# Values of three last expert tiles over the matrix engine, half of the output sums on TensorE and ScalarE, and moved spreads, scale and stores

## What is computed

```python
h = layernorm_gamma_beta(real(fft2(maxpool2(relu(pointwise(depthwise_conv7(x)))))))   # (4, 512, 192)
h = h + linear_attention_taylor2(layernorm(h))                                        # 12 heads of 16
z = layernorm(h)
probs = softmax(z @ Wg + bg)                      # 8 experts, top-1
ffn   = top_p * (gelu(z @ W1[e] + b1[e]) @ W2[e] + b2[e])
v     = clip(ffn @ Wv + bv, -3, 3)                # one value per token
mask  = scores >= 204th largest of sigmoid(z @ Wm + bm)   # per batch, 204 = int(512 * 0.4)
gr,gi = diag((T(v) - i)^-1)                       # T tridiagonal over a batch's 512 tokens
out   = h + ffn + bk_scale * (clip([gr, gi] * mask, -10, 10) @ Wo + bo)
```

## Time and profile before

| what | us |
|---|---|
| median of 3 runs (lowest, highest) | 423.71 (422.89, 426.29) |
| the profiled execution: its own time | 424.41 |
| the profiled execution: its span | 422.5 |
| TensorE busy in the span | 374.3 (89%) |
| VectorE busy | 281.7 (67%) |
| ScalarE busy | 160.3 (38%) |
| mean granted TensorE clock | 0.931 |

### The profile page before, as it was taken

How to read it: one execution, slowest core, us unless ns; L and a number is a source line. 1 busy time by engine, 2 the same in 40 slices (tenths; PEclk the granted TensorE clock), 3 DMA queues, 4 the chain that set the end, 5 groups by cost and what they waited for, 6 DMA issues and landing times. The chain is left out here.

```text
span 422.5 us, 7775 instructions
## 1 busy us (share of the span) xinstructions
PE 374.3 (89%) x2642; PEld 252.8 (60%) x2647; DVE 281.7 (67%) x901; ACT 160.3 (38%) x321; POOL 103.3 (24%) x154
## 2 busy tenths in 40 slices
PE   7999899699998998989998889899599999997273
PEld 4476538133773354733577228798599999996251
DVE  3698843899688996886333773667426656657883
ACT  1001131595317843178531781663233443441000
POOL 2000030251303612036210262201524433421000
PEclk9999999699999999999996799999889999999555
DMA  8674049400685015810179906310511211112504
GB/s 263 193 207 147 0 130 255 125 3 2 189 223 150 2 38 155 220 52 1 55 217 247 391 2 217 115 52 16 181 32 48 53 47 53 46 40 55 168 1 149
DMA packets 26900, 47.94 MB, mean 113 GB/s; under 512 B 11044, under 2 KB 21860, under 8 KB 25332
## 3 DMA queue, kind: packets, MB, share of 16 engines
q1 hardware_dynamic: 21412, 32.73, 25.4%
q10 hardware_dynamic: 2288, 7.15, 6.7%
q0 software_dynamic: 3168, 7.65, 6.3%
HBM read 36.84 MB, written 10.68 MB: 112 GB/s over the span
## 5 line engine op out<-in xcount | busy, mean ns | idle before, releaser
L681 ACT ACTIVATE probs<-ring,ones 128x1024 f32<-128x1024 f32 (+2 forms) x72 | 66.3, 970 | 16.4 <-PE ring L1561 15.0
L606 POOL TENSOR_SCALAR_AFFINE_SELECT probs<-probs 128x256 f32<-128x256 f32 (+1 forms) x72 | 41.5, 581 | 111.2 <-ACT probs L681 111.1
L1707 PE MATMUL att<-w,probs 128*128 x276 | 49.5, 330 | 1.8 <-DVE probs L1184 1.7
L1707 PEld LDWEIGHTS att<-w,probs 128*128 128x128 f32 x276 | 44.7, 192 | 2.8 <-issue 2.7
L1561 PE MATMUL ring<-w1b 128*128 128x256 bf16 (+3 forms) x188 | 39.5, 321 | 7.5 <-ACT probs L681 3.5
L835 DVE SCALAR_TENSOR_TENSOR wide<-w,wdw,wide 128x512 f32<-128x512 f32 x60 | 44.1, 778 | 0.8
L1573 PE MATMUL att<-probs,va 128*32 128x512 f32 (+3 forms) x384 | 39.6, 454 | 2.6 <-POOL probs L606 2.1
L1561 PEld LDWEIGHTS ring<-w1b 128*128 128x128 bf16 x192 | 13.1, 101 | 38.3 <-ACT probs L681 26.5
L632 POOL DMA_INDIRECT ffn_by_token<-probs,target_i x23 | 22.3, 970 | 55.9 <-DVE probs L1193 48.0
L781 ACT ACTIVATE probs<-ring,q_area 128x128 f32<-128x128 f32 x72 | 19.9, 374 | 31.7 <-PE ring L1697 13.5
L622 POOL DMA_INDIRECT pooled<-x_by_token,source_i x23 | 22.9, 993 | 36.8 <-issue 20.6
(11 more groups left out here) (367 smaller groups left out, 707.4 us busy)
## 6 DMA issues: line engine op xcount, KB each, us to landing
w1b<-k_parts ACTq DMA_DIRECT2D x16, 384.0 KB, 10.4
w1b<-q_parts SPq DMA_DIRECT2D x16, 384.0 KB, 8.7
w<-in_w SPq DMA_DIRECT2D x1, 4608.0 KB
w1a<-in_w1a SPq DMA_DIRECT2D x1, 3072.0 KB, 11.0
w<-in_x SPq DMA_DIRECT2D x4, 512.0 KB, 3.7
w<-in_x SPq DMA_DIRECT2D x8, 256.0 KB, 5.0
q_parts<-q_area SPq DMA_DIRECT2D x12, 128.0 KB, 2.6
k_parts<-k_area POOLq DMA_DIRECT2D x12, 128.0 KB, 2.6
```

Of the source, the lines that this page charges most:

```text
L606: nc.gpsimd.affine_select(diag, diag, [[0, len(UNITS[n][1])], [1, P]], ALU.is_ge, minus_one, base=0, channel_multiplier=-1).then_inc(p_rea ...
L681: nc.scalar.activation(squares(n), bank[:, :, 0:N - P * j], ACT.Square, bias=ones[:, 0:1], scale=0.25).then_inc(sq_done, 1)
L1707: last = nc.tensor.matmul(att[2][:, 0:D], hT[slot][:, c, :], w2[:, bass.ds((e * HC + c) * D, D)], start=(c == 0), stop=(c == HC - 1))
```

## The change

It has five parts.

1. `LAST_TILES = 3`: tiles 20, 21 and 22 (before: 21 and 22) bring their values over TensorE. `IN_DRAM` becomes 20, so that the load of `v_raw` waits for one store less and the stores of three tiles stand behind its landing.
2. The three spreads stand in the iterations 18, 19 and 20 of VectorE's loop, each after that iteration's `count_higher` (before: two, in iterations 20 and 21). The third one stands ahead of the mask.
3. The scaling of `wof` moves from behind the scan's levels to the place ahead of them. A copy of one column, after a settle on VectorE's own steps, tells TensorE that `h_all` is complete (`rows_added`).
4. The ten matmuls on zeros ahead of the row product go. In their place TensorE multiplies the second halves of `h_all` by the identity into the four banks `sums_of[1, 3, 5, 7]`, and the four later products are added to that. The banks are dealt out anew.
5. VectorE adds the four first halves alone, SP stores them. ScalarE copies the four second halves out of the banks and issues their stores, two after two copies.

```diff
@@ line 52 of before @@
 YS = 4
+LAST_TILES = 3
 EARLY = TT - NT
@@ line 277 of before @@
         target_i = sb("target_i", [P, SLOT_TILES], I32)
-        lane_of, step_of = sb("lane_of", [P, 2]), sb("step_of", [P, 2])
+        lane_of, step_of = sb("lane_of", [P, LAST_TILES]), sb("step_of", [P, LAST_TILES])
         b2 = oT[:].rearrange("p g n -> p (g n)")
@@ line 312 of before @@
-        sums_of = [ring[0][:, 0, :], ring[0][:, 1, :], ring[1][:, 0, :], ring[1][:, 1, :],
-                   att[0], att[1], att[2], misc]
+        sums_of = [att[0], ring[0][:, 0, :], att[1], ring[0][:, 1, :],
+                   att[2], ring[1][:, 0, :], misc, ring[1][:, 1, :]]
@@ line 330 of before @@
         lane_ids = cnt[:].rearrange("p e t -> p (e t)")
-        own_lane = [ap[:].rearrange("p e t -> p (e t)") for ap in (incl, excl)]
-        own_value = [key[:].rearrange("p t e -> p (t e)")[:, LCH * i:LCH * i + LCH] for i in range(2)]
+        own_lane = [ap[:].rearrange("p e t -> p (e t)") for ap in (incl, excl)] + [probs[:, 3 * S:3 * S + P]]
+        own_value = [key[:].rearrange("p t e -> p (t e)")[:, LCH * i:LCH * i + LCH] for i in range(LAST_TILES)]
+        assert at + 2 * HID <= 3 * S
         assert 2 * B * CH == E * TT
@@ line 413 of before @@
         ft_done, out_ready = sem("feature_terms_done"), sem("output_ready")
+        rows_added, second_ready = sem("expert_rows_added"), sem("second_halves_ready")
@@ line 428 of before @@
-        IN_DRAM = SLOT_TILES - 2
+        IN_DRAM = SLOT_TILES - LAST_TILES
         assert SURE == 5 and SURE % 2 == 1
@@ line 473 of before @@
-        def store_out(eng, odd):
-
-            for i in range(2):
-                for b in range(odd, B, 2):
-                    eng.wait_ge(out_ready, B * i + b + 1)
-                    first = NT * b + 2 * i
-                    eng.dma_start(t["out"][P * first:P * first + 2 * P, :].rearrange("(n p) d -> p n d", p=P),
-                                  h_all[:, first:first + 2, :]).then_inc(s_out, 16)
+        def store_out(eng, first, batches):
+
+            rows = t["out"].rearrange("(b n p) d -> p b n d", p=P, n=NT)
+            tokens = h_all[:].rearrange("p (b n) d -> p b n d", n=NT)
+            for b in batches:
+                eng.dma_start(rows[:, b, first:first + 2, :], tokens[:, b, first:first + 2, :]).then_inc(s_out, 16)
@@ line 572 of before @@
                              ).then_inc(s_ffn[b], 16)
-            store_out(sp, 0)
+            for b in range(B):
+                sp.wait_ge(out_ready, b + 1)
+                store_out(sp, 0, (b,))
             sp.wait_ge(s_out, 16 * 2 * B)
@@ line 806 of before @@
             pair(LAST_PAIR, last=True)
-            store_out(act, 1)
+            for b in range(B):
+                act.wait_ge(ft_done, B + b + 1)
+                nc.scalar.activation(h_all[:, NT * b + 2:NT * b + 4, :].rearrange("p t d -> p (t d)"),
+                                     sums_of[2 * b + 1][:, 0:2 * D], ACT.Copy).then_inc(second_ready, 1)
+                if b % 2:
+                    act.wait_ge(second_ready, b + 1)
+                    store_out(act, 2, (b - 1, b))
@@ line 1255 of before @@
                     count_higher(i - SURE)
-                if i >= IN_DRAM - 1:
-                    spread(i + 1)
+                if IN_DRAM - 2 <= i < IN_DRAM - 2 + LAST_TILES:
+                    spread(i + 2)
                 if i == SURE + TT - 1:
@@ line 1305 of before @@
+            dve.wait_ge(s_wof, 16)
+            st.mark(V.tensor_scalar(wof, wof, scale3[:, 0:1], None, ALU.mult))
             for i in range(LEVELS):
@@ line 1312 of before @@
                 hb = h_all[:, NT * i:NT * i + NT, :]
-                st.mark(V.tensor_tensor(hb, hb, x2_all[:, NT * i:NT * i + NT, 0:D], ALU.add))
-
-            dve.wait_ge(s_wof, 16)
+                ins = V.tensor_tensor(hb, hb, x2_all[:, NT * i:NT * i + NT, 0:D], ALU.add)
+                st.mark(ins)
+
             dve.wait_ge(s_rows, 16)
             dve.wait_ge(s_mask, 16)
-            st.mark(V.tensor_scalar(wof, wof, scale3[:, 0:1], None, ALU.mult))
+            st.settle()
+            nc.vector.tensor_copy(nz[:, 0:1], h_all[:, 0, 0:1]).then_inc(rows_added, 1)
             st.mark(V.tensor_tensor(mask_q, mask_l[:, None, :].to_broadcast([B * CH, 4, LCH]),
@@ line 1377 of before @@
             V.tensor_scalar(f_rows, misc[:, 0:P], onecol[:, 0:1], None, ALU.add).then_inc(rows_copied, 1)
-            for i in range(2):
-                for b in range(B):
-                    dve.wait_ge(ft_done, B * i + b + 1)
-                    hb = h_all[:, NT * b + 2 * i:NT * b + 2 * i + 2, :]
-                    V.tensor_tensor(hb, hb, sums_of[2 * b + i][:, 0:2 * D].rearrange("p (t d) -> p t d", d=D),
-                                    ALU.add).then_inc(out_ready, 1)
+            for b in range(B):
+                dve.wait_ge(ft_done, b + 1)
+                hb = h_all[:, NT * b:NT * b + 2, :]
+                V.tensor_tensor(hb, hb, sums_of[2 * b][:, 0:2 * D].rearrange("p (t d) -> p t d", d=D),
+                                ALU.add).then_inc(out_ready, 1)
@@ line 1764 of before @@
             nc.tensor.matmul(att[1][:, 256:256 + LCH], both_ways, v_raw[0:B * CH, :], start=True, stop=False)
-            for i in range(2):
+            for i in range(LAST_TILES):
                 pe.wait_ge(lane_ready, i + 1)
-                last = nc.tensor.matmul(att[1][:, 256:256 + LCH], own_lane[i], own_value[i], start=False, stop=(i == 1))
+                last = nc.tensor.matmul(att[1][:, 256:256 + LCH], own_lane[i], own_value[i], start=False,
+                                        stop=(i == LAST_TILES - 1))
             last.then_inc(lanes_turned, 1)
@@ line 1786 of before @@
-            keep_clock(WARM_ROWS)
+            pe.wait_ge(rows_added, 1)
+            for b in range(B):
+                nc.tensor.matmul(sums_of[2 * b + 1][:, 0:2 * D], ident[:],
+                                 h_all[:, NT * b + 2:NT * b + 4, :].rearrange("p t d -> p (t d)"), start=True, stop=False)
             pe.wait_ge(feat_ready, 1)
@@ line 1798 of before @@
                     last = nc.tensor.matmul(sums_of[2 * b + i][:, 0:2 * D], f_rows[rows, :],
-                                            wof[rows, 2 * D * i:2 * D * i + 2 * D], start=True, stop=True)
+                                            wof[rows, 2 * D * i:2 * D * i + 2 * D], start=(i == 0), stop=True)
                     last.then_inc(ft_done, 1)
```

## The result

| | kernel before | changed kernel |
|---|---|---|
| median of 18 runs each, alternating (us) | 423.15 | 426.61 |
| ratio to before, 95% interval | | 1.0109 (1.0068 to 1.0151) |
| profiled execution: own time, span | 424.41, 422.5 | 427.26, 425.4 |
| from tile 18's take-out to the end of the span | 51.14 | 54.81 |

The change costs about 1.1%, some 4.6 us. The ratio is taken over each kernel's runs within 1.5% of its fastest run; the medians of all runs are 3.46 us (0.8%) apart. The forecast was 429.1 us, with 424.3 to 430.9 as range, and slower by over 1% as the likeliest outcome.

The account below looks back on a forecast made before the run. TensorE was taken to bound while tiles are made, VectorE behind them, the last 31 us at half clock. Terms 2.6 - 0.25 + 2.5 + 0.6 = 5.4 us on a median of 423.71 gave 429.1, range 424.3 to 430.9.

Parts of the forecast that it names:

- The whole is wrong if the time is under 427: Sign set for the whole forecast of 429.1 us: a measured time under 427 would refute it.
- Term 3 [is wrong] if the clock row shows more than 0.50 before the row product: Sign for the identity products' cost: it assumed TensorE at half clock until the row product.
- Term 1: Spreads and values of the last tiles: later mask and `v_raw` let VectorE start the lanes later, +2.6 us (1.7 to 2.8).
- takes 2.21: TensorE's down product ahead of tile 22's take-out: begins at 388.29, lasts 2.21 us, tile 22 taken at 390.75.
- so the load is late last: Ahead of the lanes: tile 22's value there by 392.7, `v_raw` used at 392.17, its load setting VectorE's start at 393.54.
- Term 2: Scaling moved ahead of the scan's levels, hidden in VectorE's wait, plus a one-column copy: -0.25 us (-0.5 to 0).
- Term 3: Identity products ahead of the row product: eight passes, 5.1 us at half clock, 2.6 hidden by the features' wait: +2.5 us.
- the first rival: TensorE's clock comes back under the identity products: +1.3 us, 425.0; chance 0.24 for early or midway.
- a rise only at the end of the identity products: Late form of the returning TensorE clock: +4.35 us, 428.1; chance 0.24 shared with the early return.
- Term 4: Output, first output product to end: last store issued after 6.1 us instead of 5.5, +0.6 us (-0.4 to +1).
- The reload of ffn: Reload behind three stores, 4.1 us later: no cost forecast; rival has it bind, up to 1.2 us, 430.3, chance 0.08.
- the spreads fit after all: Rival: VectorE's spreads make the mask late by less than a microsecond, lanes no later: +2.6 us, 426.3, chance 0.12.

Follow-up runs that it names:

- e4: Changed kernel with twenty matmuls on zeros in TensorE's wait ahead of down(22); ratio 1.0041 to the kernel before.
- e7: e6 with ScalarE's four copies in a row and the stores shared out between SP and ScalarE; ratio 0.9951 to the kernel before.
- e8: e7 with sixty matmuls on zeros in TensorE's idle time ahead of the scan; ratio 0.9956 to the kernel before.
- e5: Changed kernel with the mask ahead of the third spread and twenty matmuls on zeros ahead of down(22); ratio 1.0007 to the kernel before.
- e6: e2 with two of the four identity products in place of the fourteen matmuls on zeros ahead of the flip; ratio 0.9981 to the kernel before.
- e10: Kernel before with twenty matmuls on zeros instead of fourteen ahead of the flip; ratio 0.9973.
- e1: Kernel before with part 1 of the change alone: three tiles over TensorE, three spreads in iterations 18 to 20; ratio 1.0104.
- e11: e7 with its two spreads in iterations 18 and 20, the second behind the mask; ratio 0.9901 to the kernel before.
- e2: Changed kernel with part 1 undone: two tiles over TensorE, spreads where they were before; ratio 0.9998 to the kernel before.
- e3: Changed kernel with the mask written ahead of the third spread; ratio 1.0086 to the kernel before.
- e12: Kernel before with spreads in iterations 18 and 20, the scale ahead of the levels and twenty matmuls on zeros ahead of the flip; ratio 0.9928.
- e9: e7 with each of the eight stores cut to half its bytes; one run without a ratio, the end 4.78 us after the first store.

## Why the prediction was right, and where its terms were off

The time lies in the range and moved the way that was forecast, and the cause of the loss, three spreads in a row, is the one that was named. That the total came out near is in part luck: its misses have both signs. Two signs that the prediction had set for itself say the opposite. "The whole is wrong if the time is under 427": the median is 426.61. "Term 3 [is wrong] if the clock row shows more than 0.50 before the row product": it was 1.00 from 415.0 on, and the row product began at 415.98.

- **Term 1, the values (+2.6): right in the delays, wrong in what comes last; measured +3.48.** The 1.28 us per spread (1.27), tile 20 at +2.56 (11.67 against 9.14 behind tile 18: +2.53), the mask's delay and the issue of `v_raw` behind it all stand. What failed is the step that down(22) "takes 2.21": it takes 3.84 at half clock behind the longer wait, and with it fell the sentence "so the load is late last". Tile 22's value was last, by 0.89. I had named the dead time of VectorE there and not asked what the other wait, TensorE's, does to its clock. e4, with the clock held up, is the world of the forecast: the load binds, and the term is +2.46.
- **Term 2, scale and copy (-0.25): -0.26.** Other traces with the same two edits show the same to 0.03, but e7 and e8 show -0.04; why was not found.
- **Term 3, identity products (+2.5): +1.68.** The pass of 0.64 and the cover of 2.6 were right. The clock rose after about five of the eight passes, between the forecast and the first rival. In e5 it rose before them and the term was 0.04. What decides the moment was not found: e6 and e7, with the same code up to there, have it at different moments, so part of it is no property of the kernel. The sum given for "a rise only at the end of the identity products", +4.35, is also added wrongly: 2.6 - 0.25 + 2.5 - 0.4 - 0.65 is 3.8, since the -0.65 takes the place of term 4. That case is close to what the trace shows (3.67).
- **Term 4, the output (+0.6): wrong in mechanism.** The time of the last store's issue does not set the end; 1.5 MB at about 310 GB/s behind the first store does. By that the term is the shift of the first store alone, by my estimate zero at half clock (no run has the changed output at half clock); measured -0.72 (and -0.51 for the row product). The clock is enough to explain both, since e10 has -0.80 and -0.51 without the changed output.
- **The reload of ffn** was hidden, as worked out: VectorE shows no wait for it in the changed kernel.
- **Rivals.** That the spreads fit after all is refuted for three tiles (e1) and true for two (e11). A clock back before the identity products is seen in e5; in the changed kernel it came back under them, which the rival had as its late form.

The total, 5.4 forecast against 3.67 in the trace, is the sum of one term too small by 0.9 and others too large by 0.8 (term 3) and 1.8 (term 4 and the row product). The direction rests on part 1, and e1 and e2 show that it does.

## What to carry to other kernels

An engine's idle time in a loop belongs to the single iteration: one extra piece of work in an iteration may be taken up by the next one, the same piece in iterations in a row is paid in full, and behind it the other engine's longer wait can cost it its clock. Before work is moved from one engine to another at a kernel's end, ask whether the stores are already transfer-bound; then only the first store's time counts. When two late things stand behind each other, test both edits together, or the one that is hidden will look worthless.

## What was not expected of the hardware

- TensorE's granted clock fell from 1.00 to 0.50 after a wait of 2.54 to 2.65 us that came soon after another of 1.0 (changed kernel, e1 and e3), and did not where the wait was filled (e4, e5) or 0.8 long (the kernel before). In each case it fell just about where work began again, so it cost 1.6 us on a product of 2.2.
- The Trainium skill ("TensorE: Matmul & The Clock Gate", Part 1: The HAM clock gate) says that sustained activity releases the throttle. The runs agree, with matmuls on zeros (e10, ahead of the flip) as with real data (the changed kernel, under the identity products). The number of matmuls on zeros did not decide the moment: behind twenty the clock was up at the flip in e10 (4.03 us of them) and not in e12; behind fourteen it was not in the kernel before (3.15 us) and was in e5 (2.98 us).
- Eight stores of 192 KB from on-chip memory, the last one issued 2.5 to 3.4 us behind the first on two queues, end 6.7 to 6.9 us after the first issue in every trace; half the bytes end 4.8 us after it (e9).
